# Two-layer GNN with residual and layer norm: groups of scatters on GpSimd tied to the progress of the dense node pairs

## What is computed

```python
def egnn_conv(x, src, dst, edge_attr, W_msg, W_edge, W_root, b):
    msg = x[src] @ W_msg + edge_attr @ W_edge
    agg = segment_max(msg, dst, num_segments=x.shape[0])
    agg = where(isneginf(agg), 0.0, agg)          # nodes without an edge
    return agg + x @ W_root + b

c1 = leaky_relu(egnn_conv(x,  src, dst, edge_attr, W1_msg, W1_edge, W1_root, b1))
c2 = leaky_relu(egnn_conv(c1, src, dst, edge_attr, W2_msg, W2_edge, W2_root, b2))
out = layernorm(x + c2)                           # per node, over 96 features
```

## Time and profile before

| | |
|---|---|
| median of 3 runs | 1247.58 us (1247.06 to 1248.21) |
| the profiled execution | 1251.49 us |
| its span, first to last instruction | 1249.4 us |
| mean granted clock of TensorE | 0.740 of full |
| busy: PE, PE weight load | 1013.9 us (81%), 679.5 us (54%) |
| busy: DVE, ACT, POOL | 815.3 us (65%), 694.5 us (56%), 939.2 us (75%) |
| DMA | 248.91 MB, mean 199 GB/s |

### The profile page before, as it was taken

How to read it: one execution, slowest core, us unless ns; L and a number is a source line. 1 busy time by engine, 2 the same in 40 slices (tenths; PEclk the granted TensorE clock), 3 DMA queues, 4 the chain that set the end, 5 groups by cost and what they waited for, 6 DMA issues and landing times. The chain is left out here.

```text
span 1249.4 us, 16863 instructions
## 1 busy us (share of the span) xinstructions
PE 1013.9 (81%) x4312; PEld 679.5 (54%) x4312; DVE 815.3 (65%) x1861; ACT 694.5 (56%) x1685; POOL 939.2 (75%) x986
## 2 busy tenths in 40 slices
PE   3676667678999999828888888888888888999990
PEld 1233334345666666516666666666666665666660
DVE  4223233246877877719778878888877788777771
ACT  2333334256666666606666666666666667666661
POOL 7777777777777777777777777777777777777775
PEclk9878787797555555559888888888888889555555
DMA  8989988967767767746566656566656654777741
GB/s 232 360 276 303 310 271 272 316 174 221 215 207 224 212 210 223 226 105 175 161 159 160 160 160 160 159 161 160 159 161 165 164 146 144 222 207 216 221 132 62
DMA packets 106086, 248.91 MB, mean 199 GB/s; under 512 B 26656, under 2 KB 27552, under 8 KB 105992
## 3 DMA queue, kind: packets, MB, share of 16 engines
q1 hardware_dynamic: 67432, 161.21, 43.3%
q0 software_dynamic: 31360, 48.23, 16.0%
q10 hardware_dynamic: 7200, 38.40, 7.9%
HBM read 141.94 MB, written 105.80 MB: 198 GB/s over the span
## 5 line engine op out<-in xcount | busy, mean ns | idle before, releaser
L430 PEld LDWEIGHTS ps_z<-wr,c1t 97*128 97x128 f32 x1568 | 303.8, 276 | 135.3 <-issue 119.0
L430 PE MATMUL ps_z<-wr,c1t 97*128 97x96 f32 x1568 | 299.4, 357 | 5.9 <-DVE yo L739 5.9
L420 PE MATMUL ps<-xtb,wr 97*96 97x512 f32 x392 | 303.8, 870 | 0.0
L570 ACT ACTIVATE yo<-yo,shift,rstd 128x96 f32<-128x96 f32 x654 | 243.7, 456 | 0.5 <-DVE shift L713 0.5
L252 POOL DMA_INDIRECT out<-nat,end_i x196 | 189.3, 966 | 59.7 <-issue 40.8
L252 POOL DMA_INDIRECT agg_table<-nat,end_i x196 | 188.7, 963 | 59.7 <-issue 48.4
L241 POOL DMA_INDIRECT g_dst<-in_x,own_i x196 | 187.9, 959 | 59.8 <-issue 59.8
L241 POOL DMA_INDIRECT g_src<-agg_table,src_i x196 | 186.9, 954 | 59.8 <-issue 59.5
L241 POOL DMA_INDIRECT g_src<-in_x,src_i x196 | 185.7, 947 | 61.1 <-issue 58.6
L697 DVE TENSOR_TENSOR_SCAN mx<-mask,mx,ps_m 96x512 f32<-96x512 f32 x96 | 122.2, 1272 | 150.7 <-PE ps_m L410 149.5
L732 DVE TENSOR_TENSOR c1t<-ps,c1t 96x512 f32<-96x512 f32 x196 | 134.2, 685 | 78.4 <-ACT c1t L544 78.2
(11 more groups left out here) (58 smaller groups left out, 1188.4 us busy)
## 6 DMA issues: line engine op xcount, KB each, us to landing
xtb<-in_xt SPq DMA_DIRECT2D x98, 384.0 KB
agg_table<-zero ACTq DMA_DIRECT2D x50, 750.0 KB
xn<-in_x SPq DMA_DIRECT2D x97, 384.0 KB, 3.2
out<-yo SPq DMA_DIRECT2D x97, 384.0 KB, 3.6
mask<-mask_row SPq DMA_DIRECT2D x98, 192.0 KB, 4.6
root_keep<-rt SPq DMA_DIRECT2D x49, 192.0 KB, 4.4
rt<-root_keep SPq DMA_DIRECT2D x49, 192.0 KB
xe<-in_eat SPq DMA_DIRECT2D x98, 64.0 KB
```

Of the source, the lines that this page charges most:

```text
L420: nc.tensor.matmul(ps_1[0:D, h, :], wr1[:, :], xtb[:, k, half(h)], start=True, stop=True).then_inc(d_1, 1)
L430: last = nc.tensor.matmul(ps_z[:, h, row(j)], c1t[:, q % 2, cols(h * HJ + j)], wr2[:, :], start=True, stop=True)
L570: last = nc.scalar.activation(yo[:, q % YR, row(j)], yo[:, q % YR, row(j)], ACT.Identity, bias=shift[:, q % 2, j:j + 1], scale=rstd[:, q % ...
```

## The change

Before a group of scatters is issued, POOL now waits until `d_c1` has reached a count that grows with the number of the group. This is done at both places, for groups 2 to 48. In the first the thresholds spread the stage's 35 pairs over 49 groups; in the second they spread the 24 pairs behind LATE over FREE = 35 groups, and are held at all 98 pairs from there on. `scatter` itself is as it was.

```diff
@@ -31,6 +31,7 @@
 NM = 33
 VROWS = 2
 AHEAD = 4
+FREE = 35
 LAND = 8
 CLEARS = 40
@@ -265,6 +266,8 @@
             pool.wait_ge(s_cleared, 16 * NZ)
             for c in range(NCH):
+                if c >= 2:
+                    pool.wait_ge(d_c1, 2 * (NA + (c - 1) * NS // NCH))
                 scatter(table, c, sc_t, a_nc)
             for c in range(RD - SEAM, RD):
                 gather(x, own_i, c, g_dst, c, l_dst)
@@ -288,6 +291,8 @@
                 pool.wait_ge(s_stored, nc.gpsimd.value_load(pair_i[P - 1:P, last:last + 1], min_val=1, max_val=NQ))
                 pool.sem_inc(s_under, 1)
                 pool.wait_ge(s_under, c + 1)
+                if c >= 2:
+                    pool.wait_ge(d_c1, 2 * min(NQ, LATE + (c - 1) * (NQ - LATE) // FREE))
                 scatter(out, c, sc_o, e_done)
             for k in range(LAND):
                 pool.wait_ge(sc_o[k], 16 * ((NT + LAND - 1 - k) // LAND))
```

## The result

The changed kernel takes 1307.83 us (median of 4 runs, 1306.84 to 1309.02) against 1247.45 us (1247.06 to 1248.21): ratio 1.0483, 95% interval 1.0467 to 1.0499, 60.4 us more. The forecast was 1306.3.

The account below looks back on a forecast made before the run. POOL's queue was taken as the bound: 2.3 (second edge stage later) + 56.1 (group 4's hold) + 0.3 (restart) = 58.7 us, added to the 1247.6 us median for 1306.3 us, range 1299 to 1313.

Parts of the forecast that it names:

- POOL's queue is the bound: Whole kernel: POOL's back-to-back indirect DMAs set the end; 980 of them make about 1240 us, the span.
- Group 4 decides, 56.1 us: Output scatters: group 4's wait for the 152nd maximum is the largest difference, 56.1 us; no later wait holds POOL.
- the median should be 1247.6 + 58.7: Final sum: the cost of 58.7 us added to the median of the kernel before, giving 1306.3 us.
- The table stage, 2.3 us: Table scatters: three or four early holds on line 732 leave POOL about 2.3 us later, restart included.
- The second edge stage's delay, 2.3 us: Second edge stage: starts 2.3 us later as nothing covers the table hold; delay taken as 2.3, bounds 0 and 5.
- The restart, 0.3 us: POOL after a blocked output wait: restarting costs 0.3 us, between 0 and some 0.6.
- Met waits, 0: Some 88 of the 94 added waits hold nothing and cost 0, bounds 0 and 0.6 us.
- The scatters behind, 228.4 us: Output stage from group 4 on: the 180 scatters left run as before, 228.4 us from first start to last end.
- Rival 3: Output scatters get cheaper away from the dense work and the end comes sooner than before; chance 0.01.
- rival 1: Hand-over near 1058 us: PE's clock stays at 1.00, so the change costs 56.9 us, 1304.5 us; chance 0.05.
- The list of waits: Profile after: line 252 waits on DVE line 732 at the output, about 48 us before group 2, then two shorter.
- what is given back: While POOL is held, about 1001 to 1068 us: no other engine waits for a DMA there, so nothing is credited.

Follow-up runs that it names:

- One wait: Against the kernel before: a single new wait, for 152 maxima ahead of group 4 of the output scatters, no table waits; 1306.16 us, ratio 1.0476.
- all waits met: The changed kernel with all 94 waits kept, each for a count of only 2; 1247.29 us, ratio 1.0000 to the kernel before.
- first batch: Four variants of the changed kernel, measured where the kernel before takes 1247.31 us; they took 1247.29 to 1306.16 us.
- the experiment with table waits only: The changed kernel with the waits at the output taken out again; 1248.58 us, ratio 1.0011 to the kernel before.
- group 36: The changed kernel without table waits and with output waits from group 36 on only; 1291.92 us, ratio 1.0354 to the kernel before.
- third batch: Three variants and the changed kernel, measured on the first batch's chip where the kernel before takes 1827.74 us; the changed kernel took 1622.19 us.

## Why the prediction was right, and where its sizes were off

- **POOL's queue is the bound**: right. One wait reproduces the whole cost.
- **Group 4 decides, 56.1 us**: the group was right. In the changed kernel's own trace its wait opened at 1069.14 (1068.45 + 0.69), 1.3 us later than the 1067.8 of before. At unheld pace from 987.87 us (16 scatters of 1.264) POOL would have been there at 1008.1 instead of 1011.7; in the kernel with all waits met it was there at 1008.5. The difference is 61.0, not 56.1. Of the 4.9 us between them, 1.3 are the later opening, for which the forecast has the term of the second edge stage; 3.6 are POOL's earlier arrival.
- **The step that was mis-sized, "the median should be 1247.6 + 58.7"**: the profiled execution of before took 1251.49 us, 4 us over the median, and its output scatters began at 991.35. They began at 987.87 in the changed kernel and at 987.8 in the one with all waits met. I took the differences from that long execution and added them to the median. But in the changed kernel POOL is re-timed by a maximum on DVE, so time that POOL lost before group 4 is no longer in the end: 3.4 us were missing. The end itself was right to take from the profile: last start near 1298 forecast, 1296.1 measured.
- **The table stage, 2.3 us**: 0.7 of hold in the profiled execution, 1.1 in the experiment, and one hold instead of the three or four that I expected. DVE's 16th maximum ended at 303.93 there, 2.0 us sooner than in the earlier trace rows. The waits did not do that: it ended at 303.9 in the kernel with one output wait too, and at 305.9 in the other two kernels of the first batch without a hold at the table. It differs by 2 us from one execution to the next, which is the size of the term.
- **The second edge stage's delay, 2.3 us**: 1.3 us at the 152nd maximum, by the two profiled executions. The stage began 0.2 us earlier than in the long execution of before and ran 489.9 instead of 488.4 us. That comparison can't show the cause: the 152nd maximum ended anywhere from 1065.0 to 1069.1 us in the six traces of this condition. The firm figure is the 1.3 us of the experiment with table waits only.
- **The restart, 0.3 us**: 0.76 us at the output (1069.14 to 1069.90; the same at groups 2 and 3, 0.77 with one wait, 0.77 with group 36). Too low by 0.5. At the table it was 0.28, no more than the ordinary gap.
- **Met waits, 0**: right, 0.0 us for 94 (at most 1.1).
- **The scatters behind, 228.4 us**: 180 took 227.1 us, (1296.1 - 1069.9)/179 = 1.264 each. Rival 3 fell: the 54 with no other engine at work have the same median, 958 ns, as all 180. The Trainium skill (SBUF — State Buffer, the "DVE blocks DMA" trap) says that a DVE instruction in a two-port mode keeps GpSimd from writing descriptors. The two medians show no such price here; whether any of DVE's instructions beside these scatters runs in that mode, no run shows.
- **The clock**: rival 1 fell as well; the clock went to 1.2 GHz just ahead of the 152nd maximum again. The rule in the Trainium skill (TensorE: Matmul & The Clock Gate, Part 1), that activity releases the throttle, does not fit the stretch of 147 us with PE 1.00 busy at a granted clock of 0.50, here as in the trace of before.
- **The list of waits** did not name DVE's line for the output holds, as I had said it would, and the first of them was 53.8 us and not 48, by the same earlier arrival of POOL.

The sum for the profiled span, by what was measured: 56.1 + 1.3 (later opening) + 0.8 (restart) - 1.3 (scatters behind) = 56.9, measured 57.0 (1306.4 - 1249.4). The other 3.4 of the 60.4 us are the long profiled execution of before. The forecast's closeness is luck in part: 3.4 us missing at the median and 0.5 at the restart stand against 1.0 too much for the edge stage and 1.3 for the scatters behind, which leaves 1.6; it was 1.5 too low. The high end of its range adds up to 1312.6, not 1312.7, which changes nothing.

What the forecast did not see at all is the other condition. It credited nothing for what is given back, on rows of one execution in which scatters in full flow hold up no other engine. No row told that this could be otherwise at another time.

## What to carry to other kernels

If one queue is busy from start to end, a wait put into it costs the largest lateness of what it waits for, once. List, for every instance, the event that opens the wait against the start that it holds up, and take the maximum. If the wait re-times the queue, take the end from the event that releases it and add it up in absolute time; don't add a difference from one execution to the median of others.

Holding one queue back pays or costs by whether that queue disturbs the others, and that can differ between two times on the same chip. The waits to try are those that hold next to nothing where all goes well. The waits at the table are of that kind: 1.3 us at 1247, and nearly the same waits, one pair later, gave ratios of 0.916 and 0.910 in the other condition. Those at the output are not, at 60 us. Lowered by ten pairs they gave 0.971 and 0.970 there. At 1247 us that version was not measured; in the trace with all waits met, every one of its opening maxima ends at least 17 us before POOL gets there, so by estimate it would cost nothing. The table waits together with the lowered output waits were not tried in either condition.

## What the runs showed of the hardware

- Behind a hold at the output, the indirect DMA starts 0.76 to 0.77 us after the end of the DVE instruction that releases it; behind a hold at the table, 0.28 us. The length of the hold is not the reason. In the third batch's trace of the changed kernel, a hold of 19 us at the table restarts in 0.28 us, and one with 0.9 us of idle time at the output takes 0.76. Why the place matters is open.

```profile
361.10 0.69 DVE L737 TENSOR_TENSOR c1t<-ps,c1t 96x512 f32<-96x512 f32 x1 [0.40 <-ACT c1t L549]
362.07 0.96 POOL L253 DMA_INDIRECT agg_table<-nat,end_i  x1 [18.76 <-DVE c1t L737]
...
1439.58 0.69 DVE L737 TENSOR_TENSOR c1t<-ps,c1t 96x512 f32<-96x512 f32 x1 [0.46 <-ACT c1t L549]
1441.03 0.96 POOL L253 DMA_INDIRECT out<-nat,end_i  x1 [0.90 <-issue]
```

- 94 waits on another engine's count that are met cost POOL nothing that can be measured (ratio 1.0000, 0.9991 to 1.0009).
- The same kernel took 1247 and 1828 us on one chip, 27 minutes apart. In the second condition (traced on another chip, with output waits only) 189 indirect DMAs in a row let 3 maxima through in 240 us, at a DMA share of 0.18.
